# Q's two halves go to DRAM once per pair and come back to the stack in three transfers per batch

## The chip, the cores and the metric

The kernel runs on one core of one Trainium2 chip. The metric is device time in microseconds (us) of the whole program, the median of several runs. The engines are PE (TensorE), DVE (VectorE), ACT (ScalarE), POOL (GpSimd) and SP (SyncE, which here only waits and issues transfers).

## The reference

Cross attention followed by a quantised feed-forward network, on 16 batches of 128 rows and 1024 columns:

```python
x = x + _L0_xattn_ref(_layernorm(x), ctx_4096, ctx_4096, Wq, Wk, Wv, Wo)   # 32 heads of 32, 8 KV heads
x = x + _L0_ffn_ref(_layernorm(x), w_gate, s_wgate, w_up, s_wup, w_down, s_wdown, inv_gate, inv_up, inv_inter)
# inside attention
q = (query @ Wq).reshape(b, sq, 32, 32).transpose(0, 2, 1, 3)
scores = jnp.einsum('bhqd,bhkd->bhqk', q, k) * scale      # softmax, then @ v, then @ Wo
```

## The kernel before

The 16 batches are worked in 8 pairs. Weights and activations stand as a high and a low float16 part, and a product is three matmuls (high x high, high x low, low x high). The scores get the same precision in one matmul of depth 96: `q_stack` holds the rows high, low, high of Q on partitions 0-31, 32-63 and 64-95, and `k_stack` holds high, high, low of K; partition 96 takes the negated row maxima, through `max_dram`.

Three stages overlap by one pair each. `steady(nxt, cur, prv)` projects K, V and Q of the next pair (`k`, `v`, `xt`, `q`, PE lines 421 to 459), does attention of the current one (`s` L478 for row maxima, `mt`, `st` L496, `pv` L508 and L512), and the output projection and feed-forward of the previous one (`wo_` L531, `tq`, `gu`, `ti`, `dn`). `start` runs pairs 0 and 1 in, `finish` runs pair 7 out. Each engine runs its own list of calls in program order, and the lists are written out by hand. Only semaphores tie them.

A pair's Q is made in four items, `q0` to `q3`. ACT writes the high part (`hi`, L888), DVE the low part (`lo`, L1123) into `q_st["hi"]` and `q_st["lo"]`, each 128 partitions x 2 batches x 1024 values. The partition is 32 x (group g) + d. Then SP copies, per batch, with `fill_q` (L307 to L317): four groups times (high, low, high), twelve transfers of 32 partitions x 2 KB, from on-chip memory to on-chip memory. `fill_k` (L287) does the same with K, twelve transfers of 16 KB. SP's list in `steady` is: contexts and residual of the neighbours, `fill_k(cur, 0)`, `fill_q(cur, 0)`, `load_x(nxt, 0)`, `save_max`, `load_x(nxt, 1)`, `fill_max`, `load_res(prv, 1)`, `fill_v(cur, 0)`, `fill_k(cur, 1)`, `fill_v(cur, 1)`, `fill_q(cur, 1)`, `save_max`, `fill_max`. In `finish` the order for the second batch is `fill_q(last, 1)` and then `fill_k(last, 1)`.

`fill_q(cur, 0)` waits for the low part of `q3` and for the last `st` of the batch before. PE's `s(cur, b, 0)` (L478) waits until K and Q of that batch have landed; before `s(cur, 0, 0)` PE has six pieces of `wo_(prv, 0, ...)`, 36 matmuls. I call the batches by r = 2 x pair + b, so r is even for the first batch of a pair. In the loop of `steady` the waits of SP carry the line of the helper `passed`, L204.

Of the kernel before, what the change touches and what calls it, by code (L numbers as in the profile page):

```python
# [62 lines left out]
def build(nc, x, ctx_t, wq, wk, wv, wo, w_gate, w_up, w_down,  # L63
          s_wgate, s_wup, s_wdown, inv_gate, inv_up, inv_inter, max_dram, out):
    with ExitStack() as stack:
# [3 lines left out]
        def sem(name):  # L69
            return stack.enter_context(nc.semaphore(name))  # L70
# [55 lines left out]
        scale = sb("scale", [P, 3], F32)  # L126
        rscale = sb("rscale", [P, 3], F32)

        bank1 = [stack.enter_context(nc.psum_tensor(f"bank1_{i}", [P, 512], F32)) for i in range(2)]
        bank_s = [stack.enter_context(nc.psum_tensor(f"bank_s{i}", [P, 512], F32)) for i in range(2)]  # L130
        bank_o = stack.enter_context(nc.psum_tensor("bank_o", [P, 512], F32))
# [22 lines left out]
        xn_ready = sem("xn_ready")  # L154
        k_stacked = sem("k_stacked")
        q_stacked = sem("q_stacked")
        v_stacked = sem("v_stacked")
        s_full = sem("s_full")
        mt_full = sem("mt_full")
# [37 lines left out]
        def needed(value):  # L197

            return not isinstance(value, int) or value > 0
# [41 lines left out]
        @block.sync  # L241
        def _(sp):
            def load_piece(n):
                earlier = [m for m in range(n) if slot_of[m] == slot_of[n]]
                if earlier and earlier[-1] < NSPLIT:
                    sp.wait_ge(w_lo, earlier[-1] + 1)
                if earlier and earlier[-1] >= NSPLIT:
                    sp.wait_ge(w_hi, earlier[-1] + 1)
                sp.dma_start(slots[slot_of[n]], weights[n][0]).then_inc(w_loaded[slot_of[n]], 16)

            def load_ctx(p, b):

                if needed(N1 * (p - 1) + S1[f"x{b}1"] + 1):
                    sp.wait_ge(s1_full, N1 * (p - 1) + S1[f"x{b}1"] + 1)
                    passed(sp, p)
                sp.dma_start(inp[b][:, :], ctx_t[2 * p + b]).then_inc(ctx_loaded[b], 16)

            def load_x(p, b):

                sp.wait_ge(ctx_split, 2 * p + b + 1)  # L260
                passed(sp, p)
                sp.dma_start(inp[b][:, :], x[2 * p + b]).then_inc(x_loaded[b], 16)

            def save_max(p, b):
                r = 2 * p + b
                sp.wait_ge(mt_out, r + 1)
                passed(sp, p)
                sp.dma_start(max_dram, max_rows[:, :]).then_inc(max_saved, 16)

            def fill_max(p, b):  # L270

                r = 2 * p + b
                sp.wait_ge(max_saved, 16 * (r + 1))
                passed(sp, p)
                sp.dma_start(q_stack[SPLIT:SPLIT1, :, :, :].rearrange("p g t n -> p (g t n)"),
                             max_dram.rearrange("h n -> (h n)").rearrange("(o n) -> o n", o=1)).then_inc(max_stacked, 16)

            def load_res(p, b):

                if needed(16 * p):  # L280
                    sp.wait_ge(stored[b], 16 * p)
                    passed(sp, p)
                if is_first(p):
                    sp.wait_ge(w_hi, NW)
                sp.dma_start(x2[b][:, :], x[2 * p + b]).then_inc(res_loaded[b], 16)

            def fill_k(p, b):  # L287
                r = 2 * p + b
                sp.wait_ge(s1_free, N1 * p + S1["k1"] + 1)
                passed(sp, p)  # L290
                if needed(8 * r):
                    sp.wait_ge(st_full, 8 * r)
                    passed(sp, p)
                for g in range(4):
                    rows = slice(HD * g, HD * g + HD)
                    for i, h in enumerate(("hi", "hi", "lo")):
                        sp.dma_start(k_stack[HD * i:HD * i + HD, g, :, :], k_st[h][rows, b, :, :]).then_inc(k_stacked, 16)  # L297

            def fill_v(p, b):
                sp.wait_ge(s1_free, N1 * p + S1["v1"] + 1)  # L300
                passed(sp, p)
                if needed(2 * (2 * p + b)):
                    sp.wait_ge(pv_full, 2 * (2 * p + b))
                    passed(sp, p)
                sp.dma_start(v_cur[:, :], v_st[:, b, :]).then_inc(v_stacked, 16)

            def fill_q(p, b):  # L307
                r = 2 * p + b
                sp.wait_ge(s1_free, N1 * p + S1["q3"] + 1)
                passed(sp, p)  # L310
                if needed(8 * r):
                    sp.wait_ge(st_full, 8 * r)
                    passed(sp, p)
                for g in range(4):
                    rows = slice(HD * g, HD * g + HD)
                    for i, h in enumerate(("hi", "lo", "hi")):
                        sp.dma_start(q_stack[HD * i:HD * i + HD, g, :, :], q_st[h][rows, b, :, :]).then_inc(q_stacked, 16)  # L317

            def load_rows():
                for dst, src in ((inv_sb[0], inv_gate), (inv_sb[1], inv_up), (invi_sb, inv_inter),  # L320
                                 (sgu_sb[0], s_wgate), (sgu_sb[1], s_wup), (sd_sb, s_wdown)):
                    sp.dma_start(dst[:, :], src.partition_broadcast(P)).then_inc(rows_loaded, 16)

            def start():
                load_ctx(0, 0)
                load_ctx(0, 1)
                for n in range(0, 4):
                    load_piece(n)
                load_x(0, 0)
                load_x(0, 1)  # L330
                for n in range(4, 7):
                    load_piece(n)
                fill_k(0, 0)
                for n in range(7, 13):
                    load_piece(n)
                load_ctx(1, 1)
                load_piece(13)
                load_piece(14)
                load_ctx(1, 0)
                load_piece(15)  # L340
                load_piece(16)
                fill_v(0, 0)
                fill_q(0, 0)
                load_piece(17)
                load_piece(18)
                load_x(1, 0)
                save_max(0, 0)
                load_piece(19)
                fill_max(0, 0)
                for n in range(20, 24):  # L350
                    load_piece(n)
                load_x(1, 1)
                fill_k(0, 1)
                fill_v(0, 1)
                fill_q(0, 1)
                for n in range(24, 29):
                    load_piece(n)
                save_max(0, 1)
                load_piece(29)
                fill_max(0, 1)  # L360
                load_piece(30)
                load_piece(31)
                load_rows()

            def steady(nxt, cur, prv):
                load_ctx(nxt, 0)
                load_res(prv, 0)
                load_ctx(nxt, 1)
                fill_k(cur, 0)
                fill_q(cur, 0)  # L370
                load_x(nxt, 0)
                save_max(cur, 0)
                load_x(nxt, 1)
                fill_max(cur, 0)
                load_res(prv, 1)
                fill_v(cur, 0)
                fill_k(cur, 1)
                fill_v(cur, 1)
                fill_q(cur, 1)
                save_max(cur, 1)  # L380
                fill_max(cur, 1)

            def finish(last):
                fill_k(last, 0)
                load_res(last - 1, 0)
                fill_q(last, 0)
                load_res(last - 1, 1)
                save_max(last, 0)
                fill_v(last, 0)
                fill_max(last, 0)  # L390
                fill_q(last, 1)
                fill_k(last, 1)
                save_max(last, 1)
                fill_max(last, 1)
                load_res(last, 0)
                fill_v(last, 1)
                load_res(last, 1)

            run(sp, start, steady, finish)
            for b in range(2):  # L400
                sp.wait_ge(stored[b], 16 * PAIRS)

        @block.tensor
        def _(pe):
# [60 lines left out]
            def s(p, b, g):  # L465

                r = 2 * p + b
                if g == 0:
                    pe.wait_ge(k_stacked, 192 * (r + 1))
                    pe.wait_ge(q_stacked, 192 * (r + 1))  # L470
                if g < 2:
                    if needed(8 * r - 1 + g):
                        pe.wait_ge(exp_done, 8 * r - 1 + g)
# [404 lines left out]
        def _(act):  # L878
            def hi(p, name):
# [3 lines left out]
                    if needed(192 * 2 * p):  # L883
                        act.wait_ge(k_stacked, 192 * 2 * p)
                if name[0] == "q":
                    if needed(192 * 2 * p):
                        act.wait_ge(q_stacked, 192 * 2 * p)
                nc.scalar.activation(dst, src, ACT.Copy, scale=1.0 if name[0] == "x" else UNSCALE).then_inc(s1_hi, 1)  # L888

            def exp(p, b, g):  # L890
# [694 lines left out]
```

## Time and profile before

| | us |
|---|---|
| median of 3 runs (783.48 to 785.12) | 784.54 |
| span of the profiled execution | 782.1 |
| PE busy | 694.3 (89%) |
| DVE busy | 570.1 (73%) |
| ACT busy | 271.4 (35%) |
| POOL busy | 216.2 (28%) |
| DMA queue of SP, share of 16 engines | 25.9% |

A busy share is an average over three very different stretches: the start, where weights come in (to about 125 us), the steady loop with a period of about 85 us, and the last pair (from about 640 us). What an edit is worth has to be read where its wait ends. In the views below, a number in square brackets behind a row is the engine's idle time before that row and what ended it; "x2" merges two rows; "SPq" is SP's queue issuing a transfer, and the time in that row is the issue alone, not the transfer.

### The profile page before, as it was taken

The numbers are of one execution on the slowest core, as the hardware profiler recorded it, in microseconds if no ns is written. First come the engines' busy times: TensorE is split into PE (matmuls) and PEld (weight loads), VectorE is DVE, ScalarE is ACT, GpSimd is POOL, SyncE is SP. The second block draws the span as 40 slices with busy tenths as digits, with TensorE's granted clock in tenths as the row PEclk, the third lists the DMA queues.
The fourth block names the chain that finished last, engine by engine and source line by source line (L and its number), as shares of the span: only waits on it lengthen the run. The fifth ranks groups of instructions, "written<-read, shape, count | busy, mean of one in ns | idle before, by whom it ended". The sixth has DMA issues, their size and how long they took to land.

```text
span 782.1 us, 13916 instructions
## 1 busy us (share of the span) xinstructions
PE 694.3 (89%) x5072; PEld 426.2 (54%) x5072; DVE 570.1 (73%) x820; ACT 271.4 (35%) x417; POOL 216.2 (28%) x170
## 2 busy tenths in 40 slices
PE   3866889999999999999999999999999999758843
PEld 2753475457755675467655775557646764333321
DVE  4744564699758975898669975897679966886663
ACT  4542344143414343233315342333314340433230
POOL 3020100442142503242244204241234213232331
PEclk9995799999999999999999999999999999989985
DMA  7465468411232232222141223213232003112000
GB/s 295 145 219 180 128 194 258 115 35 52 88 100 70 52 109 78 88 57 79 47 121 50 60 85 100 67 51 108 70 95 54 31 20 112 46 52 78 1 27 27
DMA packets 36256, 71.24 MB, mean 91 GB/s; under 512 B 8816, under 2 KB 17008, under 8 KB 36208
## 3 DMA queue, kind: packets, MB, share of 16 engines
q1 hardware_dynamic: 33920, 62.42, 25.9%
q0 software_dynamic: 2304, 8.39, 2.8%
q8 instruction: 20, 0.33, 0.2%
q14 instruction: 12, 0.10, 0.0%
HBM read 44.43 MB, written 8.52 MB: 68 GB/s over the span
## 4 chain that ended last, share of the span: by engine, by line
PE 54%; DVE 16%; issue 13%; POOL 6%; SPq 4%; DMA 3%; ACT 3%; DVEq 0%; POOLq 0%; ACTq 0%
PE bank L459 20%; PE bank L531 13%; PE bank L567 4%; POOL xs L1462 3%; PE bank L421 3%; PE bank_s L478 3%; PE bank_o L508 2%; PE bank L589 2%; POOL rstd L1447 2%; DVE neg_max L1160 2%; PE bank_d L512 2%; DVE amax L1197 2%; PE bank_s L496 2%; SPq L317 2%; SPq L297 2%
## 5 line engine op out<-in xcount | busy, mean ns | idle before, releaser
L459 PE MATMUL bank<-act_t_hi,wq_hi 128*128 128x256 f16 x512 | 140.6, 275 | 2.5 <-DVE act_t_lo L1123 2.1
L459 PE MATMUL bank<-act_t_hi,wq_lo 128*128 128x256 f16 x512 | 140.4, 274 | 0.0
L459 PE MATMUL bank<-act_t_lo,wq_hi 128*128 128x256 f16 x512 | 140.3, 274 | 0.0
L1160 DVE TENSOR_REDUCE neg_max<-bank_s 128x4 f16<-128x512 f32 x128 | 82.4, 684 | 46.5 <-PE bank_s L478 46.3
L1169 DVE RECIPROCAL o_norm<-bank_d 128x512 f32<-128x512 f32 x32 | 107.3, 3353 | 12.2 <-PE bank_d L512 11.1
L1467 POOL TENSOR_TENSOR o_t_lo<-o_norm,o_t_hi 128x512 f16<-128x512 f32 x32 | 40.0, 1250 | 220.2 <-ACT o_t_hi L912 220.2
L898 ACT ACTIVATE probs<-bank_s 128x512 f32<-128x512 f32 x128 | 71.6, 596 | 78.6 <-PE bank_s L496 48.1
L531 PE MATMUL bank<-wo_hi,o_t_hi 128*128 128x512 f16 x256 | 97.4, 380 | 0.8 <-POOL o_t_lo L1467 0.8
L531 PE MATMUL bank<-wo_hi,o_t_lo 128*128 128x512 f16 x256 | 97.1, 379 | 0.0
L531 PE MATMUL bank<-wo_lo,o_t_hi 128*128 128x512 f16 x256 | 97.0, 379 | 0.0
L1462 POOL TENSOR_TENSOR xs<-xb,inv_up 128x1024 f32<-128x1024 bf16 x16 | 34.3, 2141 | 110.8 <-ACT code_g L947 110.8
L926 ACT COPY q_t<-bank 128x1024 f16<-128x1024 f16 (+1 forms) x48 | 41.6, 867 | 64.4 <-PE bank L550 45.6
L459 PEld LDWEIGHTS bank<-act_t_hi,wq_hi 128*128 128x128 f16 x512 | 50.2, 98 | 17.3 <-issue 5.9
L1447 POOL TENSOR_TENSOR rstd<-veps,minus_half 128x1 f32<-128x1 f32 x32 | 22.6, 815 | 123.5 <-DVE veps L1140 123.5
L421 PE MATMUL bank<-act_t_hi,wk_hi 128*128 128x256 f16 x128 | 37.1, 290 | 19.4 <-DVE wk_lo L1258 12.4
L459 PEld LDWEIGHTS bank<-act_t_lo,wq_hi 128*128 128x128 f16 x512 | 50.3, 98 | 7.2
L459 PEld LDWEIGHTS bank<-act_t_hi,wq_lo 128*128 128x128 f16 x512 | 50.2, 98 | 6.2
L496 PE MATMUL bank_s<-q_stack,k_stack 97*128 97x512 f16 x128 | 42.1, 390 | 8.5 <-DMA q_stack<-max_dram 4.4
L478 PE MATMUL bank_s<-k_stack,q_stack 96*128 96x128 f16 x512 | 42.7, 224 | 7.6 <-issue 2.9
L1123 DVE SCALAR_TENSOR_TENSOR q_st_lo<-bank,q_st_hi 128x512 f16<-128x512 f32 x32 | 22.0, 687 | 37.6 <-ACT q_st_hi L888 37.6
L1442 POOL TENSOR_TENSOR act_t_lo<-inp,act_t_hi 128x1024 f16<-128x1024 f32 x16 | 34.6, 2182 | 37.1 <-ACT act_t_hi L940 37.1
L478 PEld LDWEIGHTS bank_s<-k_stack,q_stack 96*128 96x128 f16 x512 | 34.1, 99 | 19.5 <-issue 6.5
(107 smaller groups left out, 1292.8 us busy)
## 6 DMA issues: line engine op xcount, KB each, us to landing
inp<-in_ctx_t SPq DMA_DIRECT2D x16, 512.0 KB, 4.8
inp<-in_x SPq DMA_DIRECT2D x16, 512.0 KB, 3.4
q_stack<-q_st_hi SPq DMA_DIRECT2D x128, 64.0 KB, 2.0
x<-in_x SPq DMA_DIRECT2D x16, 512.0 KB, 4.8
out<-x POOLq DMA_DIRECT2D x16, 512.0 KB, 3.0
q_stack<-q_st_lo SPq DMA_DIRECT2D x64, 64.0 KB, 2.0
x<-in_wo SPq DMA_DIRECT2D x6, 512.0 KB, 3.8
x<-in_wq SPq DMA_DIRECT2D x4, 512.0 KB, 6.5
```

The lines of the kernel that those rows point to most:

```text
L421: ins = nc.tensor.matmul(bank[:, 0:2 * P], wk_sb[a][:, kc, c, :], act_t[m][:, kc, :, :].rearrange("p b n -> p (b n)"), start=(kc == 0 and ...
L459: ins = nc.tensor.matmul(bank[:, :, jj, :], wq_sb[a][:, 2 * item + jj, kc, :], act_t[m][:, kc, :, :], start=(kc == 0 and (a, m) == PARTS[0 ...
L478: ins = nc.tensor.matmul(bank_s[g % 2][:, j * P:(j + 1) * P], q_stack[0:SPLIT, g % 4, g // 4, j * P:(j + 1) * P], k_stack[0:SPLIT, g % 4, ...
L496: ins = nc.tensor.matmul(bank_s[g % 2][:, :], k_stack[0:SPLIT1, g % 4, g // 4, :], q_stack[0:SPLIT1, g % 4, g // 4, :], start=True, stop=True)
L531: ins = nc.tensor.matmul(bank3[idx % 2][:, :], o_t[a][:, b, c // REP, c % REP, :], wo_sb[m][:, c, n * 512:(n + 1) * 512], start=(c == 0 an ...
L898: nc.scalar.activation(probs[:, g % 4, :], bank_s[g % 2][:, :], ACT.Exp, scale=SM_SCALE).then_inc(exp_done, 1)
L926: nc.scalar.copy(q_t[:, 0:n, :].rearrange("p c n -> p (c n)"), bank[:, 0:n * P]).then_inc(qt_ready, 1)
L1160: nc.vector.tensor_reduce(neg_max[:, c:c + REP], bank_s[g % 2][:, :].rearrange("p (j n) -> p j n", j=REP), AX_X, ALU.max, negate=True).the ...
L1169: nc.vector.reciprocal(o_norm[:, :], bank_d[:, :]).then_inc(recip_done, 1)
L1447: nc.gpsimd.tensor_tensor(dst[:, b:b + 1], veps[:, b:b + 1], minus_half[:, :], ALU.pow).then_inc(done, 1)
L1462: nc.gpsimd.tensor_tensor(xs[:, :], xb[:, :], inv_sb[u][:, :], ALU.mult).then_inc(xs_ready, 1)
L1467: nc.gpsimd.tensor_tensor(o_t["lo"][:, b, t, :, :].rearrange("p j n -> p (j n)"), o_norm[:, :], o_t["hi"][:, b, t, :, :].rearrange("p j n ...
```

## The change

Each pair's `q_st["hi"]` and `q_st["lo"]` are stored whole to a new DRAM tensor, 512 KB each. Then each batch's stack is filled from there by three transfers of 256 KB, each 32 partitions x 4 groups x 2 KB. `fill_q` waits for the two stores to have landed (`q_spilled`) in place of `q3`. PE waits for 48 counts per batch in place of 192. ACT may overwrite `q_st["hi"]` when the stores have landed, not when the fills have. The stores stand directly ahead of `fill_q(., 0)` on SP's list in all three stages.

```diff
+        q_dram = nc.dram_tensor("q_dram", (2, PAIRS, P, 2, NT * REP * P), F16, kind="Internal").ap()
...
+        q_spilled = sem("q_spilled")
...
+            def spill_q(p):
+                sp.wait_ge(s1_free, N1 * p + S1["q3"] + 1)
+                passed(sp, p)
+                for h in range(2):
+                    sp.dma_start(q_dram[h, p], q_st[("hi", "lo")[h]][:, :, :, :].rearrange("p b t n -> p b (t n)")).then_inc(q_spilled, 16)
+
             def fill_q(p, b):
                 r = 2 * p + b
-                sp.wait_ge(s1_free, N1 * p + S1["q3"] + 1)
+                sp.wait_ge(q_spilled, 32 * p + 32)
                 passed(sp, p)
                 if needed(8 * r):
                     sp.wait_ge(st_full, 8 * r)
                     passed(sp, p)
-                for g in range(4):
-                    rows = slice(HD * g, HD * g + HD)
-                    for i, h in enumerate(("hi", "lo", "hi")):
-                        sp.dma_start(q_stack[HD * i:HD * i + HD, g, :, :], q_st[h][rows, b, :, :]).then_inc(q_stacked, 16)
+                for i, h in enumerate((0, 1, 0)):
+                    sp.dma_start(q_stack[HD * i:HD * i + HD, :, :, :].rearrange("p g t n -> p g (t n)"),
+                                 q_dram[h, p, :, b].rearrange("(g d) n -> d g n", g=4)).then_inc(q_stacked, 16)
...
+                spill_q(0)
                 fill_q(0, 0)
...
                 fill_k(cur, 0)
+                spill_q(cur)
                 fill_q(cur, 0)
...
                 load_res(last - 1, 0)
+                spill_q(last)
                 fill_q(last, 0)
...
-                    pe.wait_ge(q_stacked, 192 * (r + 1))
+                    pe.wait_ge(q_stacked, 48 * (r + 1))
...
-                    if needed(192 * 2 * p):
-                        act.wait_ge(q_stacked, 192 * 2 * p)
+                    if needed(32 * p):
+                        act.wait_ge(q_spilled, 32 * p)
```

## Rows read from the trace of the kernel before

**Rows 1.** One period: PE, PEld, DVE, ACT, POOL busy, clock, DMA share, GB/s
```profile
383.70:468.90 85.20, 83.40 (x637) 52.31 (x636) 68.35 (x100) 29.63 (x49) 26.83 (x20) 1.00 0.25 76
```

**Rows 2.** Chain that ended last, around r = 10: start, length, what
```profile
475.69 7.88 PE bank L531 x36
483.57 0.58 PE bank_s L478 x8
...
490.50 0.61 DVE x L1179
```

**Rows 3.** SP's issues in order of time, fill of r = 10: start, length, what
```profile
472.34 0.59 SPq L297 DMA_DIRECT2D k_stack<-k_st_lo  x1
473.75 0.51 SPq L317 DMA_DIRECT2D q_stack<-q_st_hi  x1
...
481.28 0.59 SPq L317 DMA_DIRECT2D q_stack<-q_st_hi  x1
```

**Rows 4.** DVE in order of time, same place
```profile
472.78 0.69 DVE L1123 SCALAR_TENSOR_TENSOR q_st_lo<-bank,q_st_hi 128x512 f16<-128x512 f32 x1 [1.84 <-ACT q_st_hi L888]
...
483.96 1.29 DVE L1160 TENSOR_REDUCE neg_max<-bank_s 128x4 f16<-128x512 f32 x2 [4.12 <-PE bank_s L478]
```

**Rows 5.** Transfers of the q fill of r = 10, issue to landing
```profile
DMA to landing us min/median/max: 1.9/2.0/3.4
```

**Rows 6.** PE's waits, 186 to 640 us, all that name a transfer
```profile
PE bank_s L478 <- DMA q_stack<-q_st_hi: 0.3, 1, 0.3
```

**Rows 7.** Issue to landing: x load of 512 KB; store of 512 KB from POOL; 8 KB store
```profile
DMA to landing us min/median/max: 3.1/3.1/3.1
...
DMA to landing us min/median/max: 3.0/3.0/3.0
...
DMA to landing us min/median/max: 1.3/1.4/2.6
```

**Rows 8.** DMA alone: a store (1.45 us), an x load (2.0 us), q fill (7.8 us, 40 slices)
```profile
q0 software_dynamic: 144, 0.52, 87.9%
...
GB/s 164 246 82 246 164 82 328 0 246 82 246 492 328 410 410 410 410 410 410 328 492 492 246 328 410 410 492 410 246 573 164 164 410 82 0 0 82 0 0 0
...
GB/s 0 221 116 0 147 179 11 95 210 32 63 221 53 0 221 116 0 147 179 11 105 200 32 63 221 53 0 221 116 0 168 158 11 105 200 32 63 221 53 0
```

**Rows 9.** Other transfers near the fills: POOL's store, SP's residual load in the last pair
```profile
477.36 0.57 POOL L1479 DMA_DIRECT2D out<-x  x1 [0.65 <-POOL x L1476]
643.35 0.59 SPq L285 DMA_DIRECT2D x<-in_x  x1
```

**Rows 10.** r = 0, in the start: SP's last q issue, and the chain's first s
```profile
60.16 0.59 SPq L317 DMA_DIRECT2D q_stack<-q_st_hi  x1
...
63.70 0.24 PE bank_s L478 x4
```

**Rows 11.** First q issue of r = 2 and its last; chain there (idle is "issue")
```profile
133.49 0.54 SPq L317 DMA_DIRECT2D q_stack<-q_st_hi  x1
140.41 0.59 SPq L317 DMA_DIRECT2D q_stack<-q_st_hi  x1
...
141.45 1.08 issue
```

**Rows 12.** r = 1, in the start: last q issues, and the chain across PE's idle
```profile
98.24 0.59 SPq L317 DMA_DIRECT2D q_stack<-q_st_hi  x1
...
98.59 1.78 issue
```

**Rows 13.** r = 15, in the last pair: PE, then DVE, in order of time
```profile
693.11 0.40 PE L478 MATMUL bank_s<-k_stack,q_stack 96*128 96x128 f16 x4 [1.69 <-DMA k_stack<-k_st_lo]
...
695.50 4.28 DVE L1160 TENSOR_REDUCE neg_max<-bank_s 128x4 f16<-128x512 f32 x7 [0.57 <-PE bank_s L478]
```

**Rows 14.** r = 9, an odd batch in the loop: last q issue, PE's first s
```profile
434.72 0.59 SPq L317 DMA_DIRECT2D q_stack<-q_st_hi  x1
...
437.72 0.61 PE L478 MATMUL bank_s<-k_stack,q_stack 96*128 96x128 f16 x8
```

## The prediction

> **What bounds the kernel now.** I read the loop first, by a stretch of one period, because the start and the last pair are short. In 85.20 us PE is busy for 83.40 at full clock [rows 1], so nearly any delay put in front of PE is added to the period. Then the chain of work that ended last, around the first scores of a pair's first batch (r = 10). It is PE without a gap: dn, pv, 36 matmuls of wo, and then s at 483.57 [rows 2]. The question is who releases that s. The low part of q3, the last piece of Q, starts on DVE at 472.78 and takes 0.69, so it is ready at 473.47 [rows 4]; SP issues the first of the twelve q copies at 473.75 and the last at 481.28 [rows 3], and a copy takes 2.0 from issue to landing [rows 5]. So Q lands at 483.3, and PE's s begins some 0.2 later, at the moment at which PE runs out of wo. The path q3, SP, q_stack is 9.5 long (473.75 to 483.3) and has no slack to speak of; in the whole loop PE's waits show only 0.3 us on a q transfer [rows 6]. The order of wo and s makes the two arrive together. DVE's next work hangs on it too: it idled 4.12 before its first maximum [rows 4]. An odd batch is different: at r = 9 the last q copy is issued at 434.72 and has landed at 436.7, and PE comes to s at 437.72 out of its own work [rows 14]. A faster fill gains nothing there.
>
> So the edit has a price on the even batches, and can pay only in three other places, where the copies' 0.63 us each on SP's queue hold something up.
>
> **The new path of an even batch, step by step.**
> (1) Two stores of 512 KB. A store of 8 KB takes 1.4 from issue to landing [rows 7]. A store of 512 KB keeps 16 engines at 87.9% for 1.45 us [rows 8], that is 1.27 us of each engine, and two take 2.5. Together 3.9. The store that POOL issues lands after 3.0 [rows 7], which leaves 1.7 beside its data and would give 4.3. I take 3.9, since SP issues these as it does the 8 KB one.
> (2) Hand-over on SP: landing, wait, wait on st, issue. From q3's end to the first issue, the same two waits, it is 0.3 today (473.47 to 473.75) [rows 3, 4]. I take 0.3.
> (3) Three fills of 256 KB from DRAM. A load of 512 KB takes 3.1 [rows 7]; its data flows at 410 GB/s in most slices [rows 8], 1.28 us, so 1.8 to 1.9 is fixed. The open price is the rate of the 786 KB that follow. The copies of today, on 32 partitions each, never show more than 221 GB/s in a slice of 0.2 us [rows 8]; the transfers on 128 partitions show 410. At 221 it is 3.6 us, at 410 it is 1.9. The new fills also write 32 partitions each, one after the other, so I take 3.6, and the fill is 5.5 (lower end 3.8).
> Sum: 3.9 + 0.3 + 5.5 = 9.7, with ends 8.0 and 10.1, against 9.5 today. The issue of three transfers lies beside their data.
> (4) Collisions. Today the copies are paced by SP and the DMA engines are half idle, so other transfers slip in. The new path is paced by data. POOL's store of the previous pair is issued at 477.36 [rows 9], 3.6 after the first q issue, and moves its 1.27 us per engine about when the fills begin. I take half, 0.6 (0 to 1.3).
> So each of the five even batches of the loop's pairs 2 to 6 lands 0.2 + 0.6 = 0.8 later, and PE, DVE and all behind s shift with it: 5 x 0.8 = 4.0.
> For r = 2 today's path is shorter, 133.49 to 140.41 + 2.0, or 8.9, and PE already idled 1.08 for it [rows 11]; no store of POOL is near. 9.7 - 8.9 = 0.8 more.
> For r = 14 SP issues a residual load of 512 KB at 643.35, ahead of the q path [rows 9]; it takes 1.27 of the stores' time, and POOL's store is probably through before the fills start. 0.2 + 1.2 = 1.4 more.
> For r = 0 Q lands at 62.2 and s starts at about 63.6 out of PE's k work [rows 10]; 0.8 later is still in time, no cost. The weight pieces behind it on SP's queue leave a little earlier; I count nothing.
> Loss: 4.0 + 0.8 + 1.4 = 6.2.
>
> **Where it gains.** r = 1: the last copy is issued at 98.24, and PE idles 1.78 from 98.59 [rows 12]. The new fill has no store ahead of it and needs 5.5 in place of 12 issues and 2.0, so it lands some 3.5 earlier, before PE comes. All 1.7 is gained; next late is PE's own transposes. r = 15: in the last pair the q copies stand ahead of the k copies on SP, and PE waits 1.69 for k [rows 13]. With three issues in place of twelve the k copies start some 5.5 earlier and that wait goes. But DVE's idle before the maxima that follow is 0.57 only [rows 13]: it is busy with the quantisation until then and paces the scores. I count 0.6. Odd batches in the loop: 0.
>
> ACT's new wait, on the stores in place of the fills, is weaker than the old one and costs nothing: the stores of a pair are waited for before either fill. Behind the new wait on SP stand load_x, then save_max, which waits for maxima that come after s anyway. In the loop nothing there is hurried.
>
> Net: 6.2 - 1.7 - 0.6 = +3.9 on the profiled 782.1, which lies 2.4 under the median. Forecast 784.5 + 3.9 = 788.4.
>
> A page of the Trainium skill bears on step (3): "SBUF — State Buffer", section "Door 1: The DMA port swizzle", says that a transfer's speed goes by how many of 16 ports its partitions reach, that 32 partitions reach only 8, and gives 189 GB/s for them at 1 MiB. The trace agrees in kind, 221 against 410 [rows 8]. By the page's 189 the fill would be an estimated 0.6 longer, which over seven even batches would make it about 792.5.
>
> **The rivals.**
> B, faster: the 221 GB/s of today comes from the copies' reading side or from their small size, and the merged fills run at the rate of a big load. Then the path is 3.9 + 0.3 + 3.8 = 8.0, or 8.6 with a collision, under today's 9.5, and PE never waits for it. The gain ends where PE's own work begins: 0.3 in the loop [rows 6], 0.9 at r = 2 [rows 11], and the 2.3 above: 3.5, so 781.0. For it speaks that each copy today moves 64 KB in bursts with pauses [rows 8]; against it that even in a burst the rate is half. The Trainium skill's "DMA: Bandwidth & Descriptors", section "Rules for kernel authors", tells one to coalesce small transfers, since under 64 KB one pays mostly overhead; that is this rival.
> C, given back: the delay in front of s takes time out of later waits of PE and DVE, so that half of 6.2 is felt: 784.5 + 3.1 - 2.3 = 785.3. Against it: the chain after s runs through DVE's maxima and the residual at 490.50 [rows 2], all of which shift together.
> D, much slower: the stores' landing or the read back of just written DRAM is slower than a lone transfer, by 1.5 or more per even batch, with SP standing in the wait. It decides from a path of 11 us on. Seven such batches give 10.5 on top of the sum: 788.4 + 10.5 = 798.9.
>
> **How the numbers follow.** The sum as worked out (own range 785.5 to 792, from step (4) at 0 or 1.3 and step (1) at 4.3): 0.50. B: 0.22. C: 0.15. D: 0.13. A measurement of this kernel can tell about 0.2% from no change, 1.6 us, so "same" is 783.0 to 786.1. Faster is B and a little of C: 0.24. Same is the rest of C and the low edge of the sum: 0.17. Slower: 0.59. The range goes from B's 781.0 less 1 us for gaps between PE's instructions that the waits don't show, 780.0, to 796.0, where each even batch is 1.1 worse than the sum; what lies beyond is most of D, about 0.1.
>
> **What the changed profile would show.** PE's waits in the loop get a row of s (L478) on a transfer from q_dram, five times about 0.8; if PE shows none, B holds. The time from the first store's issue to the last fill's landing should be 9.7 to 10.5 in the loop; the stores 3.9 of it. The GB/s of a stretch with fills alone should be near 220; 400 means B. PE's idle of 1.78 at r = 1 and the wait of 1.69 at r = 15 should be gone, and DVE's maxima at r = 15 should run in one row. The period in the loop should go from 85.2 to about 86. Wrong from the start would be: fills split into small packets, or an issue on SP that takes as long as its data.

## The result, and the profile after

The changed kernel takes 797.98 us (median of 4 runs, 794.37 to 799.12) beside 784.01 (782.72 to 785.12): ratio 1.0156, 95% interval [1.0106, 1.0205], so 14.0 us slower. A second comparison gave 798.06 beside 786.06, ratio 1.0160 [1.0118, 1.0201]. The forecast was 788.4 with a range up to 796: the sign was right, the size was not.

The page of the changed kernel (span 796.6), its queue and its issues:

```profile
span 796.6 us, 13860 instructions
PE 700.4 (88%) x5072; PEld 427.7 (54%) x5072; DVE 569.2 (71%) x820; ACT 271.6 (34%) x417; POOL 216.3 (27%) x170
q1 hardware_dynamic: 33920, 70.80, 28.4%
HBM read 57.02 MB, written 16.91 MB: 93 GB/s over the span
PE 48%; DVE 17%; issue 13%; DMA 9%; POOL 5%; SPq 3%; ACT 3%; DVEq 0%; POOLq 0%; ACTq 0%
q_stack<-q_dram SPq DMA_DIRECT2D x48, 256.0 KB, 4.5
q_dram<-q_st_hi SPq DMA_DIRECT2D x8, 512.0 KB, 2.7
q_dram<-q_st_lo SPq DMA_DIRECT2D x8, 512.0 KB, 3.4
```

The same instructions stand on the engines and the queue is hardly fuller. New is that transfers hold 9% of the chain that ended last, against 3% before. Where, the chain around r = 10 shows (start, length, what), the counterpart of [rows 2 to 4]:

```profile
478.76 0.70 DVE q_st_lo L1134
...
479.70 0.36 SPq L314
...
480.25 3.42 DMA q_dram<-q_st_lo
...
483.88 0.36 SPq L324
...
484.84 6.06 DMA q_stack<-q_dram
490.90 0.12 issue
491.02 0.62 PE bank_s L489 x8
```

Before, PE and the copies arrived together. Now the chain leaves PE at q3 and comes back at s. From the first store's issue to the last fill's landing it is 490.90 - 479.70 = 11.2, against 9.6 before. SP's queue there has two stores, a wait, and one group of three issues:

```profile
479.70 0.36 SPq L314 DMA_DIRECT2D q_dram<-q_st_hi  x1
480.25 0.35 SPq L314 DMA_DIRECT2D q_dram<-q_st_lo  x1
483.88 1.44 SPq L324 DMA_DIRECT2D q_stack<-q_dram  x3
```

Landings of the two stores and the first read, then of the three reads alone (minimum, median, maximum), answering [rows 5, 7]:

```profile
DMA to landing us min/median/max: 2.7/3.4/4.7
DMA to landing us min/median/max: 4.7/5.5/6.1
```

What PE and DVE make of it: PE's s of r = 10, PE's waits from 186 to 652 us that name a transfer ([rows 6] had 0.3, once), and DVE's maxima ([rows 4] had 4.12 of idle):

```profile
491.02 0.62 PE L489 MATMUL bank_s<-k_stack,q_stack 96*128 96x128 f16 x8 [1.47 <-DMA q_stack<-q_dram]
...
PE bank_s L489 <- DMA q_stack<-q_dram: 6.1, 5, 1.5
...
491.46 1.29 DVE L1171 TENSOR_REDUCE neg_max<-bank_s 128x4 f16<-128x512 f32 x2 [5.63 <-PE bank_s L489]
```

One period from r = 8's s to r = 10's, with the columns of [rows 1]: 86.50 in place of 85.20, with PE busy for the same 83.4.

```profile
401.06:487.56 86.50, 83.44 (x636) 52.32 (x635) 68.33 (x100) 29.68 (x49) 26.90 (x21) 1.00 0.28 87
```

The span cut at PE's first s of a batch, from the traces (us). "Again" are the traces of the second comparison; the forecast's terms are sorted into the same stretches.

| stretch | before | before again | after | after again | again: difference | forecast |
|---|---|---|---|---|---|---|
| start to r = 2 | 142.53 | 143.02 | 145.55 | 141.82 | -1.2 | -0.9 |
| r = 2 to 4 | 85.26 | 85.29 | 86.07 | 88.11 | +2.8 | +0.8 |
| r = 4 to 12, four periods | 340.99 | 340.82 | 345.98 | 346.44 | +5.6 | +3.2 |
| r = 12 to 14 | 85.02 | 85.02 | 87.26 | 88.58 | +3.6 | +1.4 |
| r = 14 to the end | 128.34 | 130.28 | 131.77 | 130.95 | +0.7 | -0.6 |
| span | 782.1 | 784.4 | 796.6 | 795.9 | +11.5 | +3.9 |

So the loss is in the even batches, everywhere. The two traces of the changed kernel differ by 3.7 at the start and give that back later, so single stretches outside the loop are good to some 2 us; the loop's agree within 0.5. Part of the 3.7 is a wait of PE for the read back of the row maxima of r = 1, at about 116 us: 2.2 in the first trace and 0.5 in the second. It is 2.4 and 2.6 in two of the kernels below (the stores unread, POOL's store moved) and 0.6 or less in the others and in the kernel before, so it comes and goes, and what brings it on is open.

### The profile page after: what moved, and what is told of

Read it like the earlier page. It is cut to its first block, busy times and chain, and to the rows that moved or that the text cites. A ratio compares the mean times of both kernels' runs of the same rounds, so it can differ in the third digit from the quotient of the medians.

```text
span 796.6 us, 13860 instructions
## 1 busy us (share of the span) xinstructions
PE 700.4 (88%) x5072; PEld 427.7 (54%) x5072; DVE 569.2 (71%) x820; ACT 271.6 (34%) x417; POOL 216.3 (27%) x170
## 3 DMA queue, kind: packets, MB, share of 16 engines
HBM read 57.02 MB, written 16.91 MB: 93 GB/s over the span
## 4 chain that ended last, share of the span: by engine, by line
PE 48%; DVE 17%; issue 13%; DMA 9%; POOL 5%; SPq 3%; ACT 3%; DVEq 0%; POOLq 0%; ACTq 0%
PE bank L470 19%; PE bank L542 9%; PE bank L578 5%; DMA q_stack<-q_dram 4%; POOL xs L1473 3%; PE bank_s L489 3%; DMA q_dram<-q_st_lo 3%; PE bank L432 2%; DVE neg_max L1171 2%; POOL rstd L1458 2%; PE bank_s L507 2%; DVE amax L1208 2%; SPq L300 2%; PE bank_o L519 2%; PE bank L600 2%
## 5 line engine op out<-in xcount | busy, mean ns | idle before, releaser
L507 PE MATMUL bank_s<-q_stack,k_stack 97*128 97x512 f16 x128 | 42.3, 394 | 10.1 <-DMA q_stack<-max_dram 6.7
```

What stands on the lines that cost most here:

```text
L507: ins = nc.tensor.matmul(bank_s[g % 2][:, :], k_stack[0:SPLIT1, g % 4, g // 4, :], q_stack[0:SPLIT1, g % 4, g // 4, :], start=True, stop=True)
```

## The experiments

All are edits of the changed kernel; the one with both neighbours moved carries the edit of another as well. Paths below run from the first q store or copy issued to the last fill's landing. Periods are a quarter of the way from r = 4's s to r = 12's.

**The DRAM way on odd batches only.** Even batches keep the twelve copies (`copy_q` is the old `fill_q`), and the stores follow behind them:

```diff
-                spill_q(cur)
-                fill_q(cur, 0)
+                copy_q(cur, 0)
+                spill_q(cur)
```

> The first batch of a pair is filled on chip by the twelve copies, as before the change; the stores are issued behind those copies and only the second batch is read back from DRAM by three transfers. Theory P (the path): what costs is store, wait and read back in series ahead of the first scores of a pair, 10.1 to 11.2 us in place of 9.5. Then the loop's period is back at 85.2, PE's waits there name no q transfer of the first batch, PE's idle at r = 1 stays gone, and the time is 780 to 784.5. Rival T (the traffic): the 8.4 MB written and 12.6 MB read from DRAM in the changed kernel slow other transfers and through them the start and the end. Then a good half of the loss stays, 790 or more, since all of the stores and half of the reads are still there.

Measured: 781.11 beside 786.00, ratio 0.9953 [0.9931, 0.9976]. The four periods, then the same stretch of the changed kernel:

```profile
225.75:565.82 340.07, 332.83 (x2537) 209.23 (x2538) 273.34 (x400) 118.42 (x192) 107.06 (x81) 1.00 0.29 88
```
```profile
231.62:577.60 345.98, 333.48 (x2537) 209.09 (x2537) 273.31 (x400) 118.47 (x192) 107.91 (x81) 1.00 0.28 87
```

All of the stores and half of the reads are still there (the page has 16.91 MB written to DRAM, as in the changed kernel, and 50.72 MB read in place of 57.02), and the loss is gone: it sits in the even batches' path. What is left is faster than both kernels.

**The stores put ahead of copies that don't need them.** Both stores are issued as in the change and nobody reads them; all fills are the twelve copies.

```diff
                 spill_q(cur)
-                fill_q(cur, 0)
+                copy_q(cur, 0)
```

> The two stores per pair are there at the place that the change gives them, but nobody reads them: all batches are filled by the twelve copies on chip. Theory P: the copies' path gets two more issues ahead of it, 0.55 each in the changed kernel's loop, so 9.5 becomes 10.4 to 10.6 on the seven even batches after the first, about 6 to 7 us in all: 789 to 791. The start and the last pair keep their old shape. Rival T: the stores' 2.5 us of all DMA engines delays the copies' data and neighbours beyond the issue time, 793 or more. If the copies behind the stores catch up by themselves and the added issues are hidden: 784 to 786.

Measured: 802.56, ratio 1.0224 [1.0177, 1.0271], far over the 789 to 791 of theory P, and within rival T's "793 or more", which has no upper end. SP at r = 10:

```profile
485.20 0.36 SPq L314 DMA_DIRECT2D q_dram<-q_st_hi  x1
485.74 0.34 SPq L314 DMA_DIRECT2D q_dram<-q_st_lo  x1
486.28 0.59 SPq L337 DMA_DIRECT2D q_stack<-q_st_hi  x1
...
494.38 0.59 SPq L337 DMA_DIRECT2D q_stack<-q_st_hi  x1
```

The two stores hold SP for 486.28 - 485.20 = 1.08 before the first copy, as P had it. The copies, with the stores' data beside them, take 8.69 from first issue to end of last instead of 8.12 [rows 3]: that is T's term, 0.6. Path 11.2, period 87.2, so neither theory alone gives the time. The path is 1.6 longer and the period 2.0: in this kernel's loop PE also ran at half clock for 3.4 us after its stop at r = 6 (see the last section). Here work that nobody waits for cost in full, because it was queued ahead of work that somebody waits for.

**The same traffic, no wait for it.** From pair 1 on the first batch's fill reads the pair before's data in DRAM. So the first batch of every pair works with another pair's Q; sizes and issues are as in the change.

```diff
-                sp.wait_ge(q_spilled, 32 * p + 32)
+                stale = b == 0 and not is_first(p)
+                src = p - 1 if stale else p
+                sp.wait_ge(q_spilled, 32 * src + 32)
...
-                                 q_dram[h, p, :, b].rearrange("(g d) n -> d g n", g=4)).then_inc(q_stacked, 16)
+                                 q_dram[h, src, :, b].rearrange("(g d) n -> d g n", g=4)).then_inc(q_stacked, 16)
```

> The first fill of a pair from pair 1 on reads what the pair before stored, so it waits for older stores and not for those just issued; all transfers, their sizes and the order of issue are those of the changed kernel (Q of the first batch is thus another pair's). Theory P: the path of an even batch falls from 10.1 to 11.2 to under 8.5, since 3.4 us of stores' landing and a hand-over leave the series and only the data of both remains (2.5 + 3.6 + 1.9); PE waits for no q transfer in the loop, its period is 85.0 or less, the time 780 to 786. Rival T: with the same traffic the time stays at 790 or more.

Measured: 782.67, ratio 0.9957 [0.9931, 0.9982]. SP and PE at r = 10:

```profile
470.83 0.36 SPq L314 DMA_DIRECT2D q_dram<-q_st_hi  x1
471.38 0.35 SPq L314 DMA_DIRECT2D q_dram<-q_st_lo  x1
472.14 2.12 SPq L326 DMA_DIRECT2D q_stack<-q_dram  x3
...
480.52 0.61 PE L491 MATMUL bank_s<-k_stack,q_stack 96*128 96x128 f16 x8
```

The first read is issued 0.8 behind the second store in place of 3.6, the path is 9.0 (8.2 to 9.9 over the loop, where I had expected under 8.5), and PE's s has no wait; the period is 85.15. The only thing taken away is that the reads stand behind the stores' landing, and with it goes the whole loss.

**One of the two stores taken out of the series.** From pair 1 on only the high part's store stands ahead of the first fill, the low part's behind it; the first batch's low rows are the pair before's.

```diff
-                for h in range(2):
+                for h in (range(2) if is_first(p) else range(1)):
...
-                sp.wait_ge(q_spilled, 32 * p + 32)
+                early = b == 0 and not is_first(p)
+                sp.wait_ge(q_spilled, 32 * p + (16 if early else 32))
...
                 fill_q(cur, 0)
+                spill_one(cur, 1)
```

> From pair 1 on only the store of Q's high part stands ahead of the first fill; the store of the low part is issued behind that fill, and the first batch's low rows are read from the pair before (so Q's low part of every first batch from pair 1 on is another pair's; this part of the computation is changed, sizes and traffic are not). Theory (the path is a sum, and its two stores in series are a term of 4.0 us of which one store alone is 2.7): the path of r = 8 to 12 falls from 11.2 to about 9.9, the period from 86.6 to 85.3 to 85.7, and the time from 798 to 790 to 793. Rival (the path is long because POOL's store and the reads share the engines, and a store taken from the front only moves its bytes into the reads): path 10.8 or more, period 86.3 or more, time 796 or more.

Measured: 788.60, ratio 1.0025 [1.0001, 1.0049], 1.4 under the range expected.

```profile
477.08 0.36 SPq L317 DMA_DIRECT2D q_dram<-q_st_hi  x1
479.94 1.38 SPq L328 DMA_DIRECT2D q_stack<-q_dram  x3
481.50 0.37 SPq L317 DMA_DIRECT2D q_dram<-q_st_lo  x1
```

The hand-over comes 2.86 behind the first issue in place of 4.18, the path at r = 8 to 12 is 9.2 to 9.4, and the period 85.16: a little under the 85.3 to 85.7 expected, because the path falls below the 9.6 at which PE waits at all. The rival, that the bytes only move into the reads, is out: the low store lands only 1.0 behind the last read (481.50 + 5.82 against 486.30), so much of its data flows beside them, and the path still shortens by 1.9. Against the expected 9.9 the further 0.6 is in the reads, 6.4 from first issue to last landing in place of 7.0: POOL's store is issued 0.8 behind the first read here (480.72) and 0.5 ahead of it in the changed kernel, and the first read lands at +3.3 in place of +4.7. What is left of the loss, 2.1 on the kernel before, is at r = 2 and r = 14, where PE is still idle for 1.86 and 1.75.

**Half of each store earlier.** The stores are cut by halves of the pair: `q0` and `q1` are stored ahead of the K copies, the rest behind `q3`.

```diff
+                spill_q(cur, 0)
                 fill_k(cur, 0)
-                spill_q(cur)
+                spill_q(cur, 1)
```

> The changed kernel with each store cut in two: the half made by q0 and q1 is stored ahead of the k copies, the half made by q2 and q3 at the old place, so that only 2 x 256 KB stand in series ahead of the read back. Theory P (the series of data is the price): that takes 1.27 us off the path, 8.6 to 8.8 at r = 2 and 4 and 9.7 to 10.0 at r = 8 to 12; the period goes to 85.3 to 85.6 and the time to 788 to 792. Rival R (the price is in fixed latencies, not in bytes): the path shortens by under 0.5 and the time stays at 795 or more. The added stores take about 1 us of SP's time ahead of the k copies, which wait for nothing critical.

Measured: 796.26, ratio 1.0121 [1.0075, 1.0167]: no gain to speak of. At r = 10:

```profile
472.00 0.66 SPq L314 DMA_DIRECT2D q_dram<-q_st_hi  x1
472.86 0.58 SPq L314 DMA_DIRECT2D q_dram<-q_st_lo  x1
...
480.76 0.59 SPq L300 DMA_DIRECT2D k_stack<-k_st_lo  x1
481.69 0.63 SPq L314 DMA_DIRECT2D q_dram<-q_st_hi  x1
482.49 0.62 SPq L314 DMA_DIRECT2D q_dram<-q_st_lo  x1
485.23 1.44 SPq L324 DMA_DIRECT2D q_stack<-q_dram  x3
```

The path from the late stores fell from 11.2 to 10.4 (481.69 to 492.11), but a pair of early halves holds SP 1.77 (472.00 to 473.77) ahead of the K copies, and those ended only about half a microsecond ahead of q3 before. Now they end at 481.35, q3 has been ready since 480.71, and the late stores start 0.98 behind it in place of 0.25. From q3's end to the last landing it is 11.4, as in the changed kernel. It tells nothing of the series, only that SP's queue has no room there either.

**POOL's store moved away.** POOL's store of the previous pair's second batch isn't issued by `fin` but behind POOL's next two `act_t_lo`, some 8 us later:

```diff
-                fin(prv, 1)
+                fin(prv, 1, later=True)
```

> The changed kernel with one more edit: in the loop POOL's store of the previous pair's second batch is issued after the two context subtractions of the next round, some 8 us later, when the fills of the first batch are through. Theory C (collision): at r = 8, 10 and 12 the read back starts while that store moves, the first read transfer takes 4.5 to 4.7 us in place of the 3.3 to 3.5 of r = 2 and 4, and the path is 11.0 to 11.2 in place of 9.8 to 10.1. Then with the store moved the path is 9.8 to 10.1 on all of them, the loop gains 1.1 us on each of three to five batches, and the time is 793 to 795. Rival L (the reads are slow by themselves late in the loop): path stays at 11, time within 1 us of 798.

Measured: 793.52, ratio 1.0101 [1.0056, 1.0147]. Landings of stores and reads at r = 10, and PE's waits in the loop:

```profile
DMA to landing us min/median/max: 2.7/3.6/5.0
...
PE bank_s L489 <- DMA q_stack<-q_dram: 3.2, 4, 1.3
```

The last read lands 5.0 behind its issue in place of 6.1, the path of r = 10 is 10.15 in place of 11.2, the period 85.7 in place of 86.5 and 86.6, and PE's wait is halved. The collision is real and costs about 1.0 of an even batch's path, near the 1.27 per engine that the store moves. The first trace of the changed kernel shows it without any edit: at r = 4 and 6 POOL's store stands 1.4 and 1.0 ahead of the first read and the path is 10.1 and 10.4, at r = 8 to 12 it stands 0.5 ahead and the path is 11.0 to 11.2.

**And the residual load of the last pair.** The kernel of the last experiment, with the 512 KB load issued ahead of the K copies in `finish` in place of directly ahead of the stores:

```diff
-                fill_k(last, 0)
                 load_res(last - 1, 0)
+                fill_k(last, 0)
```

> The kernel with POOL's store moved later, and in the last pair the residual load of 512 KB is issued ahead of the K copies instead of behind them, directly before Q's stores. Theory (the long path of 12.5 us at r = 14 is the residual load in the stores' time): the stores land 2.7 and 3.4 after their issue there as in the loop, the path of r = 14 falls to 10.0 to 10.7, and the time is 790.0 to 792.5 against 793.5. Rival (r = 14 is long for another reason, K copies or the state of the DRAM): path of r = 14 stays at 12 or more and the time within 1 us of 793.5.

Measured: 788.99, ratio 1.0048 [1.0022, 1.0073]. Landings of the two stores at r = 14, in the changed kernel and here:

```profile
DMA to landing us min/median/max: 5.1/5.5/5.9
```
```profile
DMA to landing us min/median/max: 2.7/3.1/3.6
```

The path of r = 14 is 9.6 in place of 12.5, PE goes to its s without a stop where it was idle for 2.58, and r = 12 to 14 takes 85.02, as before the change. The rival (K copies, or the DRAM) is out. The time fell by 4.5, more than expected. From r = 12 to r = 15 the trace gives 87.75 + 38.05 - 85.02 - 37.21 = 3.6 of it; the rest is within what such runs differ by.

**Ends only.** Copies everywhere but for r = 1 and r = 15, which are read back from DRAM (`start` and `finish` keep the store, behind their copies); the loop's part:

```diff
-                spill_q(cur)
-                fill_q(cur, 0)
+                copy_q(cur, 0)
...
-                fill_q(cur, 1)
+                copy_q(cur, 1)
```

> Twelve copies on chip everywhere but for the second batch of the first and of the last pair; only those two pairs are stored, behind the copies of their first batch. Theory P: what is gained over the kernel before comes from PE's idle at r = 1 (1.8 us) and the k wait at r = 15 (0.6 to 1.7) alone, so this equals the kernel with all odd batches from DRAM, ratio 0.994 to 0.998 to the kernel before, 781 to 784 where that is 785. Rival O (the odd batches of the loop gain too, since SP is free earlier): this is slower than the other by over 1 us.

Measured: 781.45 beside 786.06, ratio 0.9953 [0.9928, 0.9978], the same as with all odd batches. So the DRAM way gains nothing at the odd batches of the loop, and nearly the whole gain is at the two places that the prediction named (0.8 is in the loop, which here works by the old copies).

## Why the prediction was wrong in size

The order of things was right: a path of an even batch without slack, lengthened, and paid by PE nearly one for one. What failed is the size of four terms, all too small: the collision of step (4) (0.6, measured 1.1), the residual load at r = 14 (1.4, measured 2.2 and 3.6), the fills of step (3) (5.5, measured 5.9), and PE's clock after a stop, which stands nowhere in the sum.

| kernel | path r = 8, 10, 12 | period | time |
|---|---|---|---|
| before | 9.6 | 85.2 | 784.0 to 786.5 |
| after, two traces | 11.0 to 11.2 | 86.5, 86.6 | 798.0, 798.1 |
| POOL's store moved | 9.9 to 10.3 | 85.7 | 793.5 |
| both neighbours moved | 9.8 to 10.1 | 85.6 | 789.0 |
| one store in series | 9.2 to 9.4 | 85.2 | 788.6 |
| not waiting | 8.3 to 9.0 | 85.2 | 782.7 |

Point by point:

- **Step (1), two stores in series, 3.9.** Measured 3.97 (479.70 to 480.25 + 3.42), the first landing at 2.67. Right. The Trainium skill's "DMA: Bandwidth & Descriptors", section "🔬 Anatomy of one DMA — SWDGE (gpsimd) path", says for that path that about 2.0 us of a transfer are fixed and mostly the wait until the target memory confirms the last byte, longest for HBM. These are SP's stores: 2.67 less 1.27 of data [rows 8] leaves 1.4 fixed.
- **Step (2), hand-over, 0.3.** Measured 0.21 (483.67 to 483.88). Right.
- **Step (3), three fills, 5.5.** Without a neighbour they take 5.9 (481.69 to 487.58, both neighbours moved). The flow from 0.2 behind the first issue on (481.9 to 487.6, in 40 slices of 0.14 us) and SP's queue in it:

```profile
GB/s 0 0 0 0 0 43 29 57 201 216 273 287 359 287 316 244 187 201 216 201 201 201 201 172 187 201 273 259 216 144 129 72 86 43 14 0 0 0 0 0
q1 hardware_dynamic: 432, 0.79, 62.8%
```

  The data runs from about 482.7 to 486.6, near 200 GB/s on average (many slices show 201, the highest 359), so 3.9 in place of 3.6, and 2.0 is fixed in place of 1.9. The main choice, the rate of 32 partitions against that of a big load, held. The Trainium skill's 189 GB/s ("SBUF — State Buffer", "Door 1: The DMA port swizzle") would give an estimated 4.2 of data; the measured rate lies between it and my 221.
- **Step (4), the collision, 0.6 of 0 to 1.3.** This term was mis-sized. At r = 10 the fills take 7.0 (483.88 to 490.90) against 5.9 undisturbed: 1.1. I placed POOL's store 3.6 behind the first q issue, by before's clock, and took half. In the changed kernel POOL issues it at 483.34, 0.5 ahead of the first read:

```profile
483.34 0.57 POOL L1490 DMA_DIRECT2D out<-x  x1 [0.65 <-POOL x L1487]
```

  It is in nearly full collision, and the first read lands at +4.7: the path pays 1.1 of the store's 1.27. (The old path probably held a part of this: the twelve copies took 9.3 to 9.7 at r = 4 to 14, where POOL's store is near, and 8.9 at r = 2 and on the odd batches of the loop. The prediction's 0.63 per copy holds for the latter; by [rows 3] it is 0.68 at r = 10.) Together the path is 11.2 where 10.3 was forecast: +0.4 from step (3), +0.5 from step (4).
- **The loop.** Forecast 0.8 a period, measured 1.25 and 1.4: over four periods 5.0 and 5.6 in place of 3.2.
- **r = 14, +1.4.** Mis-sized too: +2.2 and +3.6 (0.5 of the 3.6 is a wait for the row maxima of r = 12, which the first trace doesn't have). I charged the residual load with its 1.27 of data. Its removal shortened the path by 2.9, more than twice that. The stores land 5.1 and 5.9 after their issue with it and 2.7 and 3.6 without. Why 1.27 of a neighbour's data costs 2.3 there isn't settled: the load was issued 0.6 ahead of the first store.
- **r = 0, no cost.** Q lands at 65.1 and 63.9 in place of 62.2 and 62.3, a path of 11.1 and 10.4 against the 9.7 of the sum. PE's first s is 1.7 later in the first trace and 0.2 in the second, so "still in time" held in one of two.
- **r = 2, +0.8.** Path 9.8 and 10.3 against 8.9. PE's idle before s was 1.08 and 0.84 before; it grew to 1.66 and 2.14, and to 2.85 in the kernel with both neighbours moved, though neither of these two is near: this stretch, with weights still coming in, moves from run to run.
- **The gains.** At r = 1 PE goes from its transposes to s without a stop, where [rows 12] had 1.78 of idle:

```profile
98.65 1.34 PE L455 MATMUL bank<-ident,inp 128*128 128x128 f32 x8
99.82 0.61 PE L489 MATMUL bank_s<-k_stack,q_stack 96*128 96x128 f16 x8
```

  The span to r = 2 fell by 2.1 in the odd-only kernel and by 2.4 in the ends-only one. It need not all be the idle: right behind it, both traces of the kernel before show PE at half clock for 3.4 us (from 100.7 and 101.2), and these two kernels show no such stretch. At r = 15 PE's wait for K is gone too, and r = 14 to 15 fell by 1.25 there, where I counted 0.6. The loop gave 0.9 and 0.8 more in the two kernels with copies. From q3's end, rather than from the first issue, Q lands 9.7 to 9.8 later there and 9.8 to 10.1 later in the kernel before, 0.6 and 1.0 less over four batches, which is about this gain; why SP starts a little sooner is open. These 4.2 are most of the 0.5% by which those kernels beat the old one.
- **Left out: the clock.** See below: 1.7 behind r = 2 and 2.4 behind r = 14, about 4 of the 11.5 in the trace again.
- **Rival C**, the delay half given back, is refuted: at r = 10 the path is 1.65 longer and the period before it 1.5.
- **Rival B**, the fills at the rate of a big load, would have taken 3.8 for them; they take 5.7 to 5.9 with both neighbours moved (r = 8 to 12).
- **Rival D** gave 798.9, nearly the measured time, and its bound, a path from 11 us on, is met. Its mechanism is refuted. The stores land as sized, and reading back what was just written isn't slow. With both neighbours moved, at r = 8 to 12, the three reads of just written data take 5.7 to 5.9; those of the odd batches there, written some 40 us earlier, take 5.7 to 6.0. First reads of the pair before's data land 5.0 after issue when three stores run beside them. The number was right by other terms: a collision in full, the residual load, the clock.

Of the 11.5 in spans I can place, over the forecast of 3.9: 2.4 in the loop, 2.2 at r = 14's path (and the wait at r = 12), 2.0 between r = 2 and 4, mostly clock, 1.3 after r = 14 (clock, less the gain at r = 15), less 0.3 at the start. The medians differ by 12.0 and 14.0; what lies between is the spread of spans and not explained.

## What to carry to other kernels

A round trip through DRAM is two landings in a row, and the second can't start before the first: here 4.2 before the first read is even issued, against copies that SP merely issues one behind the other. Use it where the store has time to land unseen (the second batch of a pair: 0.5% gained at start and end) and not on a path without slack. When a path goes from paced by issues to paced by data, place every neighbour's transfer by the new schedule, not the old, and charge what is issued ahead at least at its data: here a store 0.5 ahead of the reads cost 1.1 of its 1.27, and a load 0.6 ahead of the two stores cost 2.3, more than its 1.27. Then try to move the neighbour, which here gave back 9 of the 12 us by moving two transfers.

## What the runs showed of the hardware

- A long idle of PE inside the full-clock stretch was often followed, within 1 us of its end, by a stretch at half clock. Windows of the changed kernel's second trace (length, PE, PEld, DVE, ACT, POOL busy, clock, DMA share, GB/s) around r = 2 and r = 14:

```profile
139.00:142.10 3.10, 0.96 (x9) 0.41 (x7) 0.00 (x0) 0.00 (x0) 3.10 (x2) 0.99 0.70 167
142.10:145.50 3.40, 3.40 (x17) 1.72 (x15) 1.29 (x2) 0.00 (x0) 0.17 (x1) 0.50 0.21 81
661.00:664.30 3.30, 1.28 (x6) 0.39 (x4) 0.00 (x0) 0.00 (x0) 0.00 (x0) 1.00 1.01 217
664.30:671.10 6.80, 6.15 (x27) 3.36 (x28) 2.58 (x4) 0.00 (x0) 0.00 (x0) 0.50 0.13 47
```

  PE had been idle for 2.14 and 2.68, and then ran at 0.50 (1.2 GHz) for 3.4 and 6.8 us. It isn't certain to follow. The twelve traces have 19 idles of PE of 1.75 to 3.22 us between 95 and 675 us; 12 were followed by such a stretch and 7 were not, with both kinds found from 1.8 to 2.6 (at r = 14, with POOL's store moved, PE was idle for 2.58 and stayed at full clock). None of the 20 idles of 1.2 to 1.7 was followed by one, and no such stretch began there without an idle. Two rows behind an idle of 1.8: r = 1 in the kernel before, and r = 6 in the kernel with the stores unread:

```profile
100.70:104.10 3.40, 2.99 (x21) 2.66 (x18) 2.58 (x4) 1.82 (x3) 0.00 (x0) 0.50 0.96 319
322.30:325.70 3.40, 3.40 (x16) 1.74 (x14) 1.85 (x4) 0.00 (x0) 0.00 (x0) 0.51 0.13 53
```

  The price: r = 14 to 15 took 38.05 with POOL's store moved, and in the changed kernel 39.71 with a stretch of 3.4 us at half clock behind r = 14 (first trace) and 40.46 with one of 6.8, so 1.7 and 2.4. Likewise r = 2 to 4 took 86.1 and 86.5 without such a stretch, and 87.8 to 88.3 with one of 3.4. A wait of PE can thus cost nearly twice its length.
- Issuing a store of 512 KB to DRAM holds SP's queue in the loop for 0.54 to the next issue (0.36 of it the instruction), a little less than a copy of 64 KB. It doesn't go by bytes: a store of 256 KB, half of a pair's, held it for 0.80 (481.69 to 482.49). Two stores of 512 KB ahead of twelve copies cost 1.08, and the copies beside the stores' data 0.6 more.
